# Six of the eight additions of expert results, moved from VectorE to GpSimd

## The reference

```python
gu = jnp.einsum('th,ehj->etj', x, w_gate_up)          # the routed experts
h = _swiglu(gu, I)
y = jnp.einsum('eti,eih,te->th', h, w_down, combine)   # 2 of 16 per token
gu_s = x @ shared_gate_up                              # the shared expert
y = y + _swiglu(gu_s, SI) @ shared_down
...
x = x + _L1_attn_ref(xn, ...) + _L1_ffn_ref(xn, ...)
```

## Time and profile before

| | |
|---|---|
| median of three runs | 525.41 us |
| the profiled execution's own time | 524.41 us |
| its span | 522.60 us |
| granted TensorE clock, mean | 0.992 |
| TensorE busy | 493.8 us, 94% |
| VectorE busy | 349.0 us, 67% |
| ScalarE busy | 300.7 us, 58% |
| GpSimd busy | 277.1 us, 53% |

### The profile page before, as it was taken

How to read it: one execution, slowest core, us unless ns; L and a number is a source line. 1 busy time by engine, 2 the same in 40 slices (tenths; PEclk the granted TensorE clock), 3 DMA queues, 4 the chain that set the end, 5 groups by cost and what they waited for, 6 DMA issues and landing times.

```text
span 522.6 us, 7351 instructions
## 1 busy us (share of the span) xinstructions
PE 493.8 (94%) x2438; PEld 373.7 (72%) x2438; DVE 349.0 (67%) x735; ACT 300.7 (58%) x591; POOL 277.1 (53%) x207
## 2 busy tenths in 40 slices
PE   8999989999999999999999999999698989889995
PEld 5455546777886678888888888877566756666785
DVE  5999998999988999669889983342212222322357
ACT  4889979888999688677483352543132332323221
POOL 0033767947471864775634396437435666567500
PEclk9999999999999999999999999999979999999999
DMA  8800022005331022114004845712502222233285
GB/s 309 307 1 1 0 83 80 1 1 203 120 122 41 1 82 80 51 42 166 1 2 166 272 177 154 237 40 76 197 32 83 86 84 80 82 80 92 72 293 198
DMA packets 19956, 54.83 MB, mean 105 GB/s; under 512 B 3328, under 2 KB 5808, under 8 KB 19920
## 3 DMA queue, kind: packets, MB, share of 16 engines
q1 hardware_dynamic: 15408, 42.04, 23.3%
q0 software_dynamic: 4512, 12.33, 8.0%
HBM read 36.66 MB, written 17.74 MB: 104 GB/s over the span
## 4 chain that ended last, share of the span: by engine, by line
PE 57%; DVE 24%; issue 6%; ACT 4%; DMA 4%; POOL 3%; another core or an unknown queue 1%; DVEq 0%; SPq 0%; ACTq 0%; POOLq 0%
PE bank L303 41%; PE bank L484 8%; DVE tk L1057 3%; DVE m L1055 3%; PE bank L516 2%; DMA xg<-xn_rows,tab 2%; PE bank L543 1%; DVE tk L1063 1%; PE bank L397 1%; DVE m L1035 1%; DVE tk L1039 1%; DMA y_rows<-m_y,dest 1%; DVE hs L1183 1%; DVE hs L1173 1%
## 5 line engine op out<-in xcount | busy, mean ns | idle before, releaser
L303 PE MATMUL bank<-mw,m_xt 128*128 x188 | 64.3, 484 | 6.1 <-DVE m_y L1306 3.9
L1443 POOL DMA_INDIRECT xg<-xn_rows,tab x47 | 46.1, 980 | 41.5 <-PE bank L516 29.1
L1449 POOL DMA_INDIRECT y_rows<-m_y,dest x47 | 46.4, 988 | 29.4 <-DVE m_y L1306 17.0
L1306 DVE TENSOR_SCALAR m_y<-bank,gslot 128x256 f32<-128x256 f32 x47 | 22.3, 482 | 49.2 <-DMA y_rows<-m_y,dest 27.3
L303 PEld LDWEIGHTS bank<-mw,m_xt 128*128 128x128 f32 x188 | 35.1, 198 | 26.2 <-issue 13.3
L303 PE MATMUL bank<-yhr,wsg_h 128*128 128x512 f32 x128 | 53.0, 414 | 0.0
L1299 DVE TENSOR_TENSOR m_h<-m_h,bank 128x176 f32<-128x176 f32 x47 | 15.2, 335 | 55.6 <-ACT m_h L857 46.8
L303 PE MATMUL bank<-yhr,wsg_l 128*128 128x512 f32 x128 | 50.0, 391 | 0.0
L303 PE MATMUL bank<-hyr,wsg_h 128*128 128x512 f32 x128 | 49.9, 390 | 0.0
L303 PE MATMUL bank<-mw,m_ht 88*128 x188 | 45.9, 383 | 2.5 <-issue 2.5
L1387 POOL TENSOR_TENSOR tk<-tk 128x512 f32<-128x512 f32 x16 | 20.4, 1285 | 40.7 <-ACT tk L748 40.5
(11 more groups left out here) (263 smaller groups left out, 1404.9 us busy)
## 6 DMA issues: line engine op xcount, KB each, us to landing
mw<-in_gu SPq DMA_DIRECT2D x16, 352.0 KB
ga<-y_rows SPq DMA_DIRECT2D x8, 512.0 KB, 6.8
mw<-in_dn SPq DMA_DIRECT2D x16, 176.0 KB
wsg_w<-in_wsg SPq DMA_DIRECT2D x4, 512.0 KB, 4.7
xn_rows<-fg SPq DMA_DIRECT2D x4, 512.0 KB, 2.7
spilled_x<-fa SPq DMA_DIRECT2D x4, 512.0 KB, 3.6
hx<-spilled_x SPq DMA_DIRECT2D x4, 512.0 KB, 4.0
spilled_r<-fb SPq DMA_DIRECT2D x4, 512.0 KB, 5.5
```

What stands on the lines that cost most here:

```text
L303: mm = e.matmul(o, a, b, start=n == 0, stop=n == len(terms) - 1)
L1306: e.tensor_scalar(m_y[j % 3][:, :], ps("jd", j)[:, 0:D], gslot[:, j:j + 1], None, ALU.mult).then_inc(s["jy"], 1)
L1443: e.indirect_dma_start(out=xg[j % 3][:, :], out_offset=None, in_=xn_d, in_offset=bass.IndirectOffsetOnAxis(ap=tab[:, j:j + 1], axis=0)).th ...
L1449: e.indirect_dma_start(out=y_d, out_offset=bass.IndirectOffsetOnAxis(ap=dest[:, j:j + 1], axis=0), in_=m_y[j % 3][:, :], in_offset=None).t ...
```

## The change

VectorE's list loses combine(b, k) for b = 0, 1, 2. GpSimd's list gets them at its very end, after yput(46), in the same order, with the same operands, and counted by a new semaphore cbp. combine(3, 0) and combine(3, 1) stay where they were on VectorE, and cb now counts only these. The stores of batches 0 to 2 wait for cbp.

```diff
@@ vector @@
-            def combine(b, k):
-                r = rows_[b % 2] if b > 1 else back[b][:, :].rearrange("p (i d) -> p i d", d=D)
-                if b < 2:
-                    q.wait_ge(d_park[b], 32)
-                if b == NB - 1:
-                    q.wait_ge(d_rb[b % 2], nth(b))
-                else:
-                    q.wait_ge(s["od"], 2 * b + 2)
+                q.wait_ge(d_rb[b % 2], nth(b))
                 q.wait_ge(*d_ga[2 * b + k])
                 if k:
-                    q.wait_ge(s["cb"], 2 * b + 1)
+                    q.wait_ge(s["cb"], 1)
                 o = GA[2 * b + k][:, :].rearrange("p (i d) -> p i d", d=D)
-                e.tensor_tensor(r, o, r, ALU.add).then_inc(s["cb"], 1)
+                e.tensor_tensor(rows_[b % 2], o, rows_[b % 2], ALU.add).then_inc(s["cb"], 1)
...
                 if b == NB - 1:
-                    q.wait_ge(s["cb"], 2 * NB)
+                    q.wait_ge(s["cb"], 2)
...
-            jtimes(45); jtimes(46); jout(42); jout(43); jout(44); jout(45); jout(46); dtimes(3, 6); dlow(3, 6); combine(0, 0); dtimes(3, 7)
-            combine(0, 1); combine(1, 0); dtimes(3, 8); dlow(3, 7); dlow(3, 8); combine(1, 1); combine(2, 0); combine(2, 1); dtimes(3, 9)
+            jtimes(45); jtimes(46); jout(42); jout(43); jout(44); jout(45); jout(46); dtimes(3, 6); dlow(3, 6); dtimes(3, 7)
+            dtimes(3, 8); dlow(3, 7); dlow(3, 8); dtimes(3, 9)
             dtimes(3, 10); dlow(3, 9); dlow(3, 10); combine(3, 0); combine(3, 1); dout(3, 0); dout(3, 1)
@@ gpsimd @@
+            def combine(b, k):
+                r = rows_[b % 2] if b > 1 else back[b][:, :].rearrange("p (i d) -> p i d", d=D)
+                if b < 2:
+                    q.wait_ge(d_park[b], 32)
+                q.wait_ge(s["od"], 2 * b + 2)
+                q.wait_ge(*d_ga[2 * b + k])
+                if k:
+                    q.wait_ge(s["cbp"], 2 * b + 1)
+                o = GA[2 * b + k][:, :].rearrange("p (i d) -> p i d", d=D)
+                e.tensor_tensor(r, o, r, ALU.add).then_inc(s["cbp"], 1)
...
+            combine(0, 0); combine(0, 1); combine(1, 0); combine(1, 1); combine(2, 0); combine(2, 1)
@@ sync @@
             def store(b):
-                q.wait_ge(s["cb"], 2 * b + 2)
+                q.wait_ge(s["cbp"], 2 * b + 2)
```

More of the change, by code:

```diff
@@ L57 @@
     "exn eg ec "
-    "rt eo rcm va ohj oh rtm jx jxc ju js jh jt jtc jd jy cb"
+    "rt eo rcm va ohj oh rtm jx jxc ju js jh jt jtc jd jy cb cbp"
 ).split()
```

## The result

| | before | after |
|---|---|---|
| median of 20 runs | 525.40 us | 529.73 us |
| lowest and highest | 521.05, 527.85 | 526.17, 531.35 |
| profiled execution, its span | 524.41, 522.6 | 531.21, 529.4 |

The kernel after takes 1.0087 of the time before, 95% interval 1.0065 to 1.0108: 4.6 us more, between 3.4 and 5.7. The forecast was 528.0 with a range of 526.2 to 531.0, slower with a chance of 0.83. So the measured median lies inside the range, 1.7 above the forecast.

A forecast was written before the change was run, and what follows sets the result against it. Bound: TensorE's matmuls until 513.81, then a relay of VectorE and ScalarE. Removal 0, SP waits 0, held dlow 3.2 us: 527.6 from the profiled 524.41, 528.6 from the median 525.41, middle rounded 528.0 us, range 526.2 to 531.0.

The forecast's parts named there:

- What is removed: 0.: VectorE, last 25 us: six additions, 7.3 us in all, leave its list; none is on the path, gain 0.
- The collision and the turns: Last 25 us: VectorE operations with two SBUF inputs and GpSimd additions alternate, the one that has waited first; end moves 3.2 us.
- the walk: Step-by-step times of GpSimd's six additions against dlow(3,6) to dlow(3,9): chunk 9 starts at 518.5, not 515.24, +3.26 us.
- rival B: VectorE and GpSimd, last 25 us: same turns, but whole durations after each release; +4.1 us, 528.9; chance 0.08.
- Price of the new waits on SP: 0.: SP's queue: stores of batches 0 to 2 wait for GpSimd's additions, store(2) landing before the last halves are issued; 0 us.
- rival E: VectorE and GpSimd, last 25 us: no exclusion, dlow never held; 0 change, 524.4 to 525.4 us; chance 0.11.
- hidden: GpSimd, last 25 us: its six additions alone would end at 516.6 and add nothing to the time.
- Rival C: TensorE, chunks 9 and 10: clock falls in the new idle, their 2.9 us double; 530.9 us; chance 0.06.
- a granted clock under 1 before 519: TensorE in the profile after: a clock below 2.4 GHz before 519 us was listed as showing the forecast wrong.
- The sum: Whole kernel: 3.2 us added gives 527.6 from the profiled execution, 528.6 from the median; middle rounded, 528.0 us.
- rival A: The forecast itself: dlow waits for GpSimd's additions, end moves 3.2 us to 528.0, own range 526.9 to 529.6; chance 0.72.

The follow-up runs named there:

- the three executions with the clock up: The kernel after, unaltered, profiled three more times: tail (first load of expert results issued to end of span) 27.6 us each, against 24.2 before; ratio 1.0084.
- the first execution: The kernel after, unaltered, in its first profile: tail (first load of expert results issued to end of span) 28.7 us, against 24.2 before; ratio 1.0087.
- the write-only kernel: The kernel after with each GpSimd addition replaced by two memsets, the additions for batches 0 to 2 left out: tail 25.8 us, ratio 1.0017 to the kernel before.
- the twelve halves: The kernel after with each of GpSimd's six additions cut into two of 128x512: tail 30.8 us, ratio 1.0127 to the kernel before.
- the kernel with the late memset: The kernel before plus one GpSimd memset of 8 words a partition after the last dout, for which nobody waits: tail 29.6 us, ratio 1.0100.

## Why the prediction was right

**What is removed: 0.** Right. With GpSimd only writing, VectorE had the six additions off its list and the first dout came at the same 20.1 us.

**The collision and the turns.** Right in place, order and size. Forecast dlow rows 2.8, 2.2, 2.8 (2.85 in the walk), 1.5; measured 2.62, 2.15, 2.86, 1.46. Chunk 9 started 3.22 us late (520.76 - 2.30 - 515.24), against 3.26, and in the three executions with the clock up dout came 3.2 to 3.3 us late. TensorE's new idle was 0.74 and 1.09 in place of 1.0 and 1.35, the last, 2.22, as forecast. That is a matter of counting and not of the turns: the walk took TensorE as ready when the next matmul could have started, while the rows count from the end of the last record, 0.16 later, and the first matmul after an idle stretch is followed after 0.22 us and not 0.12. GpSimd's first landing, 0.17 earlier than assumed in the first execution, isn't the reason: in the second it came as assumed, and the idle was 0.73 and 1.09. The Trainium skill, page "SBUF — State Buffer", section "Who interferes with whom", has the rule that made this case: a VectorE instruction with two SBUF inputs contends with a GpSimd instruction that reads SBUF, not with one that only writes. Both halves are borne out here: 2.62 us against 0.69 with one input in PSUM, and 0.69 beside memsets. Read to the letter (rival B) it would be 0.9 us too long: a held dlow ended 0.56 after the release, not 0.69.

**"Price of the new waits on SP: 0."** Right for the stores (store(2) was issued at 520.18, 5.9 before the last halves), but the list of what is behind GpSimd's last addition was not complete: GpSimd's own closing DRAIN is. It costs 0.2 us in the tail when the clock stays up, and nothing when it falls; it would have shown even without any collision. By the prediction's own sum the six additions alone end at 516.6, 18.2 us into the tail; 8.0 us more is 26.2, an estimate (the write-only kernel, whose last memset ended at 17.8, had 25.8). So rival E, called 0 change, would have been about 2.0 us slower, and "hidden" was wrong for the six additions.

**Rival C, the clock, 0.06.** Too low, and its condition wrong. It was argued away because 2.2 us of idle is shorter than the 3.38 of the earlier trace rows; in one of four executions the clock was down after 2.22 us, with 0.74 and 1.09 before it, for 15 of 24 matmuls, at 1.4 us and not the full 2.9. It fell after 2.42 us with the twelve halves too, and stayed up after 2.22 and 2.23 us in the other three. In the first execution this was one of the prediction's own signs of being wrong: "a granted clock under 1 before 519" (520.76 is 518.46 in the times of before). The four executions are of the same kernel, and in the three without the fall the path up to dout was the one forecast.

**The sum.** The shift of 3.2 us was right, the time less so: the sum from the median was 528.6, and 528.0 is it moved halfway towards the single profiled execution. 3.2 us were forecast; the tails say 3.4 (three of four) or 4.5 (one), a mean of 3.7. The measured 4.6 (3.4 to 5.7) and 4.3 (3.0 to 5.6) on the second chip agree with that. Their middle lies 0.6 to 0.9 higher; whether the clock falls more often than in one of four, or the stage ahead of the tail is a little longer, is open. The two terms that the sum lacked, the DRAIN and the clock, both made it longer, and 529.73 is just above rival A's own range (to 529.6): that the time stayed inside the stated range owes something to the room left at its top for rivals B and C.

## What to carry to other kernels

Before work is moved from VectorE to GpSimd, ask what its inputs are: additions from SBUF to SBUF on GpSimd take twice the time (2.37 against 1.22 us) of something that VectorE's own two-SBUF-input instructions need, so moving 7.3 us away made the rest wait. Look then at which of VectorE's remaining instructions feed the engine that bounds the stage; here GpSimd's additions held nobody whose second input came from PSUM, and its memsets held nobody. And keep GpSimd's last instruction at least 8 us ahead of the end of the program.

## What the runs showed of the hardware that was not expected

- GpSimd's closing DRAIN ended 7.7 to 7.8 us after its last operation in every kernel (after a memset of 0.10 us, one of 0.96, after additions and after the scatter), and in no kernel did the span end less than 8.0 after that operation. VectorE's own closing DRAIN, in the kernel with the late memset, lasted 1.3 us, ScalarE's 0.7. What GpSimd does in it, and whether it would be shorter in a kernel without indirect DMAs, was not tried.
- GpSimd adds a tile of 128x1024 to itself in 1.9 us, two tiles in 2.4.
- The granted clock was at 1.2 GHz after TensorE had been idle for only 2.2 us, with 1.8 us more of idle in the 7 us before, in one of four executions; and after 2.42 us in the only profiled execution of the twelve halves.
